# A four-layer graph network on one core: edge rows kept behind the node table, equal sources counted where sums to sources are made, shared segments stored in two transfers, and stores issued by ScalarE

## The reference, cut to what matters

```
L0  three times: h = h @ W_self.T + b + mean over dst of h[src] @ W_neigh.T   (relu after two of them)
L1  h = (mean over dst of (x[src]-e) @ W_O.T + mean over src of (x[dst]-e) @ W_I.T + x @ W_S.T + biases) / 3,
    then batch norm over all nodes
L2  message = h[src] @ W_msg.T + b + embedding[type], summed over dst; then a GRU cell on all nodes
L3  mean over src of (h @ W.T + b)[dst]
```

## Time and profile before

| | us |
|---|---|
| time of the kernel, median of 3 runs | 7199.35 |
| lowest and highest run | 7185.6, 7202.62 |
| the profiled execution's own time | 7203.87 |
| its span | 7202.2 |

### The profile page before, as it was taken

The page is one execution under the profiler, slowest core; times in us unless marked ns, Lnnn a source line. Parts: engine busy times, 40 slices in busy tenths (PEclk is TensorE's granted clock), DMA queues, the critical chain, the costliest instruction groups (busy, mean ns, idle before and its releaser), DMA issues. The chain is left out here.

```text
span 7202.2 us, 109209 instructions
## 1 busy us (share of the span) xinstructions
PE 4892.9 (68%) x23937; PEld 3564.2 (49%) x23937; DVE 4001.4 (56%) x14866; ACT 2898.1 (40%) x6394; POOL 4067.0 (56%) x4659
## 2 busy tenths in 40 slices
PE   4777745558788786723646536798999978844553
PEld 2455533445565565623543324576666644433553
DVE  5665555654564565733323216666999989943210
ACT  0565534443563463323001100246888855533000
POOL 0655556640550454666555650575888877755555
PEclk9888867679998998855778868557999989955776
DMA  2344446659667766934546537443444444433443
GB/s 85 126 143 135 138 142 189 192 165 333 214 223 290 240 223 206 299 127 135 155 131 145 103 50 229 132 130 131 171 171 170 171 138 147 123 104 123 81 71 47
DMA packets 730736, 1139.32 MB, mean 158 GB/s; under 512 B 109785, under 2 KB 426376, under 8 KB 730220
## 3 DMA queue, kind: packets, MB, share of 16 engines
q1 hardware_dynamic: 589770, 962.41, 40.0%
q0 software_dynamic: 140800, 175.08, 11.8%
HBM read 703.03 MB, written 456.06 MB: 161 GB/s over the span
## 5 line engine op out<-in xcount | busy, mean ns | idle before, releaser
L1061 POOL DMA_INDIRECT G_x<-node_table,G_idx x400 | 399.8, 999 | 165.6 <-issue 131.1
L1061 POOL DMA_INDIRECT G_V<-layer_rows,G_idx x400 | 381.3, 953 | 165.3 <-issue 98.0
L1915 PE MATMUL bank<-O_r,O_eq 125*125 125x128 f32 x1600 | 283.0, 359 | 242.5 <-ACT O_out L1941 210.3
L1091 PE MATMUL bank<-first_last_indicators,G_V 125*128 (+1 forms) x1600 | 282.8, 299 | 234.3 <-DVE G_V L1741 158.2
L1073 POOL DMA_INDIRECT out<-O_out,O_idx x200 | 314.4, 1572 | 211.5 <-DMA out<-O_out,O_idx 149.8
L1421 PE MATMUL bank<-B_S,B_V 127*128 127x125 f32 x2000 | 319.5, 302 | 148.2 <-DVE B_S L1409 104.6
L1073 POOL DMA_INDIRECT node_table<-H_out,H_idx x200 | 318.2, 1591 | 171.5 <-DMA node_table<-H_out,H_idx 116.0
L1915 PEld LDWEIGHTS bank<-O_r,O_eq 125*125 125x125 f32 x1600 | 275.6, 272 | 249.9 <-issue 166.7
L1091 PEld LDWEIGHTS bank<-first_last_indicators,G_V 125*128 125x128 f32 x1600 | 277.1, 261 | 244.4 <-issue 161.3
L1421 PEld LDWEIGHTS bank<-B_S,B_V 127*128 127x128 f32 x2000 | 276.2, 209 | 185.5 <-issue 154.7
L1058 POOL COPY G_idx<-i_tb 128x4 int32 (+1 forms) x100 | 18.5, 185 | 607.8 <-POOLq L255 483.6
(11 more groups left out here) (472 smaller groups left out, 15917.5 us busy)
## 6 DMA issues: line engine op xcount, KB each, us to landing
P_x<-node_table SPq DMA_DIRECT2D x196, 512.0 KB
B_V<-values SPq DMA_DIRECT2D x250, 256.0 KB
B_krow<-keys_dst SPq DMA_DIRECT2D x250, 250.0 KB
values<-G_V SPq DMA_DIRECT2D x200, 256.0 KB
BN_g<-node_table SPq DMA_DIRECT2D x195, 256.0 KB
out<-P_out SPq DMA_DIRECT2D x195, 256.0 KB
node_table<-G_xg SPq DMA_DIRECT2D x97, 512.0 KB
layer_rows<-A_a SPq DMA_DIRECT2D x100, 256.0 KB
```

What stands on the lines that cost most here:

```text
L1061: pool.indirect_dma_start(out=rows[u % len(rows)][:, c, :], out_offset=None, in_=table, in_offset=bass.IndirectOffsetOnAxis(ap=idx[u % len ...
L1091: last = nc.tensor.matmul(m.bank[7][:, bass.ds((i * TILE + c) * 2, 2)], V[0:EP, c, :], m.ind[0:EP, bass.ds(i * TILE + c, 1), :].rearrange( ...
L1915: last = nc.tensor.matmul(m.bank[2 + u % 2][0:EP, d * D:(d + 1) * D], eq[u][:, c, d * EP:(d + 1) * EP], r[u][:, c, :], start=(c == 0), sto ...
```

## The change

What it does, part by part:

1. **x1 rows behind the node table.** The table's memory grows to `XE`, 2N rows of 128 and behind them one group of 128 rows per tile, `X1`. B3's x1 is stored there in edge order by one dense transfer of 256 KB per body on SP; B3 has no POOL work any more. `i_src2` points at the source's X1 row where the source ends an edge, and at its row in the table otherwise; G3 gathers from XE. B4 loads x1 into the left half of `xg`, ACT writes g into the right half, and POOL scatters whole rows of 1 KB through `i_dstf`, so the destinations' x1 comes into the table here. Before, x1 went in B3 and g in B4, 512 B each.
2. **Equal sources.** The count behind `seen` moves from A to H. There DVE counts on the keys which H loads anyway, body by body, and writes the scatter's indices itself; POOL's index copy in H goes. `i_srcf`, which O2 uses, is made there too. A's `srow` loads go.
3. **Short stages.** Masks are taken with a stride (every fourth column, 50 at a time) so that the four tiles of a body come to lie side by side in one bank: 16 matmuls, 2 copies of 50 x 512, 2 transfers.
4. **Stores on ScalarE.** The queue that issues them changes for A's values, the layers' o (B1, B2), B3's h1 and h1T, and G4's V.
5. **Index copies.** `copy_index` is a call of its own. In A both copies stand ahead of the eight gathers. `next_index` copies the next body's index one body ahead, in G1, G2 and B5; for this it waits until the gathers of four bodies before have landed. Elsewhere the order is as before. B5's loop on POOL is unrolled 4 times instead of 8.

```diff
@@ edges_setup
-            nc.vector.tensor_scalar(m.i_src2[0:EP], csrc[:], 2.0, None, ALU.mult).then_inc(s_v, 1)
...
+            nc.vector.scalar_tensor_tensor(t1[:], csrc[:], -2.0, tb[:], ALU.mult, ALU.add).then_inc(s_f, 1)
+            dve.wait_ge(s_f, 5)
+            nc.vector.scalar_tensor_tensor(hi_f[:], t1[:], 2.0 * N, t2[:], ALU.add, ALU.mult).then_inc(s_f, 1)
+            dve.wait_ge(s_f, 6)
+            nc.vector.scalar_tensor_tensor(m.i_src2[0:EP], csrc[:], 2.0, hi_f[:], ALU.mult, ALU.add).then_inc(s_f, 1)
@@ index copies
+def copy_index(nc, index, idx, s_idx, g, w):
+    nc.gpsimd.tensor_copy(idx[w % 4][:], index[:, bass.ds(g * TILE, TILE)]).then_inc(s_idx, 1)
+def next_index(nc, f, index, idx, s_idx, g, w, landed):
+    if f.has(g):
+        f.landed(landed, g - 4, w % 4, 64)
+        copy_index(nc, index, idx, s_idx, g, w)
@@ share_segments
-                        nc.vector.tensor_copy(R[k][c][:], m.bank[4 * (1 - k) + c][0:TC, 0:D]).then_inc(s_r, 1)
+                    nc.vector.tensor_copy(R[k][:], m.bank[4 + k][0:T // TILE, :]).then_inc(s_r, 1)
...
-                    for c in range(2):
+                    for q in range(TILE):
                         for e in range(2):
-                            last = nc.tensor.matmul(m.bank[4 * (1 - k) + c][0:TC, 0:D], masks[e][:, c * TC:(c + 1) * TC],
+                            last = nc.tensor.matmul(m.bank[4 + k][0:T // TILE, q * D:(q + 1) * D],
+                                                    masks[e][:].rearrange("p (i c) -> p i c", c=TILE)[:, :, q],
...
-                            sp.dma_start(table[EP + k, c * TC // TILE:(c + 1) * TC // TILE, q, :], R[k][c][q:TC:TILE, :]).then_inc(s_out, 16)
+                    sp.dma_start(table[EP + k], R[k][:]).then_inc(s_out, 16)
@@ edges_start (A)
-                    gather(nc, pool, f, m.i_src, idx_s, s_is, i, u, a["x"], xs_whole, s_gs)
-                    gather(nc, pool, f, m.i_dst, idx_d, s_id, i, u, a["x"], xd_whole, s_gd)
+                    copy_index(nc, m.i_src, idx_s, s_is, i, u)
+                    copy_index(nc, m.i_dst, idx_d, s_id, i, u)
+                    gather(pool, f, idx_s, s_is, i, u, a["x"], xs_whole, s_gs)
+                    gather(pool, f, idx_d, s_id, i, u, a["x"], xd_whole, s_gd)
...
-                    sp.dma_start(srow[u][:], ks.to_broadcast([128, EG])).then_inc(s_sr[u], 16)
...
-                            nc.vector.scalar_tensor_tensor(hits[:, c, 0:e], srow[u][0:EP, 0:e], m.csrc[:, t], m.before[:, c, 0:e],
-                                                           ALU.is_equal, ALU.mult, accum_out=seen[:, t]).then_inc(s_c, 1)
@@ A, ScalarE (and alike in layer, third_layer, messages)
+                        Flow(act, has, m).after(s_h, i - 2)
+                        act.dma_start(value_tiles(m, i - 2), hs_whole[v][:]).then_inc(s_vo[v], 16)
@@ third_layer (B3)
+                    if has(i - 3):
+                        v = (u - 3) % 4
+                        Flow(sp, has, m).after(s_x1, i - 3)
+                        sp.dma_start(edge_rows(m.X1, i - 3), x1_whole[v][:]).then_inc(s_1o[v], 16)
...
-            @block.gpsimd
-            def _(pool):
...
-                        scatter(nc, pool, f, m.i_dst2f, idx, s_i, i - 3, (u - 3) % 4, m.XH, x1_whole, s_sc)
@@ outgoing_self (B4)
+                    Flow(sp, has, m).landed(s_sc, i - 4, u, 64)
+                    sp.dma_start(xg_whole[u][:, :, 0:D], edge_rows(m.X1, i)).then_inc(s_x[u], 16)
...
                     f.after(s_g, i)
+                    f.landed(s_x, i, u)
                     f.landed(s_sc, i - 4, u, 64)
-                    scatter(nc, pool, f, m.i_dst2f1, idx, s_i, i, u, m.XH, g_whole, s_sc)
+                    copy_index(nc, m.i_dstf, idx, s_i, i, u)
+                    scatter(pool, f, idx, s_i, i, u, m.XG, xg_whole, s_sc)
@@ add_to_src (H), VectorE
+                        f.after(s_seen, i - 1)
+                        for c in range(TILE):
+                            e = (c + 1) * EP
+                            last = nc.vector.scalar_tensor_tensor(hits[:, c, 0:e], krow[u][0:EP, 0:e], m.csrc[:, bass.ds(i * TILE + c, 1)],
+                                                                  m.before[:, c, 0:e], ALU.is_equal, ALU.mult, accum_out=seen[u][:, c:c + 1])
...
+                        f.landed(s_sc, i - 4, u, 64)
+                        nc.vector.tensor_scalar(later[u][:], seen[u][:], 0.5, float(1 << 22), ALU.is_gt, ALU.mult).then_inc(s_ix, 1)
...
+                        nc.vector.tensor_scalar(idx[u][0:EP], row[u][:], 1.0, None, ALU.add).then_inc(s_i, 1)
@@ gru (B5), GpSimd
+                    next_index(nc, g, m.i_dst, idx, s_i, i + 3, u + 3, s_x)
                     if has(i + 2):
-                        g = Flow(pool, has, m)
                         g.after(s["x2"], i - 2)
-                        gather(nc, pool, g, m.i_dst, idx, s_i, i + 2, (u + 2) % 4, m.XG, x_whole, s_x)
-
-                sweep(pool, -2, n, n + 4, body, unroll=8, back=7, ahead=2, special=0)
+                        gather(pool, g, idx, s_i, i + 2, (u + 2) % 4, m.XG, x_whole, s_x)
+
+                sweep(pool, -3, n, n + 4, body, back=7, ahead=3, special=0)
@@ network
+        m.XE = nc.dram_tensor("node_table", [2 * m.N + edge_rows_at_end, D], F32, kind="Internal").ap()
+        m.XH, m.X1 = m.XE[0:2 * m.N, :], m.XE[2 * m.N:, :]
```

More of the change, by code:

```diff
@@ L1486, in body @@
                         nc.scalar.activation(o[v][:], m.bank[2 + v % 2][:, 0:EG], ACT.Relu, bias=m.col[f"b{k}"]).then_inc(s_o, 1)
-                sweep(act, 0, n, n, body, back=5, ahead=0, special=0)
+                    if has(i - 2):
+                        v = (u - 2) % 4
+                        Flow(act, has, m).after(s_o, i - 2)
+                        act.dma_start(turned(H_out, i - 2), o[v][:]).then_inc(s_oo[v], 16)
+                sweep(act, 0, n, n + 1, body, back=5, ahead=0, special=0)
             @block.tensor
@@ L1525, in body @@
                 f = Flow(pool, has, m)
-                f.landed(s_vo, i - 4, u)
-                f.after(s_hl, i - 4)
-                gather(nc, pool, f, m.i_tb, idx, s_i, i, u, table, V_whole, s_g)
-            return 0, n, n - 1, 0, body
+                next_index(nc, f, m.i_tb, idx, s_i, i + 1, u + 1, s_g)
+                if has(i):
+                    f.landed(s_vo, i - 4, u)
+                    f.after(s_hl, i - 4)
+                    gather(pool, f, idx, s_i, i, u, table, V_whole, s_g)
+            return -1, n, n - 1, 0, body
         def sync(sp):
@@ L1655, in body @@
                         nc.scalar.activation(h1T[u][:], m.bank[4 + u % 2][:, 0:EG], ACT.Copy).then_inc(s_hT, 1)
-                sweep(act, 0, n, n + 3, body, back=8, ahead=0, special=0)
+                        Flow(act, has, m).after(s_h1, i - 4)
+                        act.dma_start(edge_rows(m.H1, i - 4), h1_whole[u][:]).then_inc(s_ho[u], 16)
+                    if has(i - 5):
+                        v = (u - 5) % 4
+                        Flow(act, has, m).after(s_hT, i - 5)
+                        act.dma_start(turned(m.HDb, i - 5), h1T[v][:]).then_inc(s_To[v], 16)
+                sweep(act, 0, n, n + 4, body, back=8, ahead=0, special=0)
             @block.tensor
@@ L1846, in _, with add_to_src @@
                 sweep(pe, 0, n, n, body, back=4, ahead=0, special=0)
-def add_to_src(nc, m, name, load, table, index, weight=None):
+def add_to_src(nc, m, name, load, table, weight=None):
     n = m.T // TILE
@@ L1861, in add_to_src @@
         idx = P.slots("idx", [128, TILE], I32)
+        if weight:
+            hits, seen = P.sb("hits", [EP, TILE, EG]), P.slots("seen", [EP, TILE])
+            later, row = P.slots("later", [EP, TILE]), P.slots("row", [EP, TILE])
+            s_seen, s_ix, s_pad = P.sem("seen"), P.sem("row"), P.sem("index_pads")
         s_l, s_e, s_k, s_sc = (P.sems(x) for x in ("r", "ea", "k", "out"))
@@ L1873, in body @@
                         sp.dma_start(ea_whole[u][:], attr_rows(m, i)).then_inc(s_e[u], 16)
-                    Flow(sp, has, m).after(s_eq, i - 4)
+                    Flow(sp, has, m).after(s_seen if weight else s_eq, i - 4)
                     keys = m.KS.rearrange("t p -> (t p)")[bass.ds(i * EG, EG)].rearrange("(a n) -> a n", a=1)
@@ L1951, in body @@
                     f.landed(s_sc, i - 4, u, 64)
-                    scatter(nc, pool, f, index, idx, s_i, i, u, table, out_whole, s_sc, add=True)
+                    if not weight:
+                        copy_index(nc, m.i_srcf, idx, s_i, i, u)
+                    scatter(pool, f, idx, s_i, i, u, table, out_whole, s_sc, add=True)
                 sweep(pool, 0, n, n - 1, body, back=4, ahead=0, special=0)
@@ L2073, in body @@
                         load(f, i + 3, (u + 3) % 4)
-                    if has(i - 4):
-                        f.after(s_v, i - 4)
-                        sp.dma_start(value_tiles(m, i - 4), V_whole[u][:]).then_inc(s_vo[u], 16)
-                sweep(sp, -3, n, n + 3, body, back=4, ahead=3, special=0)
```

(11 more changed lines are left out.)

145 lines of the change are left out of this document (62 added, 83 removed).

## The result

The changed kernel takes 7119.36 us (median of 4 runs, 7109.29 to 7132.73), the kernel before 7200.99 us beside it. The ratio is 0.9891, with a 95% interval of 0.9867 to 0.9914: 62 to 96 us faster. The forecast was 7064 us, a gain of 135 us; the measured time lies at the upper end of the range (the ratio, taken from the forecast's 7199.35 us, gives 7120.9 us), and the gain is six tenths of the one forecast. The profiled execution took 7115.8 us, its span 7114.1 us, 88.1 us less than before.

| stage | before | after | difference | forecast |
|---|---|---|---|---|
| B3 | 342.5 | 259.4 | -83.1 | -66 |
| A | 666.0 | 712.9 | +46.9 | -30 |
| five short stages | 86.9 | 58.3 | -28.6 | -24 |
| B5 | 478.3 | 444.0 | -34.3 | -21 |
| G1 + G2 | 734.5 | 703.2 | -31.3 | 0 |

A forecast was written before the change was run, and what follows sets the result against it. Each stage has its own limit: DMA bytes in B1 and B2, POOL's row of indirect transfers in A, B3 and B4, scatter landings in H. Terms -66 -30 -24 -21 +5 +2 -1 = -135 us give 7064 us, range 7020 to 7120.

The forecast's parts named there:

- One of the two long gaps becomes a short one: A: both index copies in front save POOL 0.51 us per body; taken as -16 us (0 to -26).
- PE may take part of it back: A: PE, at mean clock 0.67, needs 6.9 us a body, so the copy-order gain of 20 us was cut to 16.
- The 28.9 us of waits on ACT's h: A: POOL's waits for ACT's h, behind DVE; the count's leaving was to recover 6 us (0 to 20).
- The second term of A: A: removing the equal-source count gains 8 us in DVE's last bodies and 6 us of POOL's waits.
- the prediction's own sign: The forecast is wrong if B3 stays over 300 us, short stages don't fall, or an unchanged stage moves over 5 us.
- B3's own rate: B3: 350 transfers at 0.80 us give 279 us, 285 with ends; 276 us taken, -66 us (-88 to -42).
- The floor of 254 us: B3: at B1's 0.71 us per transfer the stage takes 254 us; with A at -50, a rival of 7022 us, 14%.
- three bodies, 17.7 us: B4: SP's slack while awaiting scatter i-4 covers the 16.1 us from first load to first scatter; +5 us (+2 to +35).
- Three bodies, 29 us, cover them: H: that slack hides DVE's new wait for scatter i-4; +2 us (-2 to +10).
- The wait for it goes: 0.53 us: B5: copying the index a body ahead saves 0.53 us in some 40 bodies, -21 us (-25 to 0).
- rival 3: B5 keeps its pace, +21 us, 7085 us, 12%; a DVE-GpSimd lock held for whole instructions would instead let DVE's wait shrink.
- rival 6: Stores block ACT where DMA is saturated in B1, B2 and B3: 7292 us, slower; 3%.

The follow-up runs named there:

- run 1: Changed kernel with A's index copies each before its own four gathers, B4 loading x1 a body later, G1's early copy undone: 7051.62 us, ratio 0.981.
- run 4: Changed kernel plus, in A, one unused small POOL copy and its wait between source and destination gathers: 7051.13 us, ratio 0.981, A 661.4 us.
- BN: The batch_norm stage, without POOL work in the changed kernel (237 us); with 160 unused gathers added: 434.4 us without gaps, 403.3 and 308.1 us with gaps.
- run 9: Changed kernel with the count back in A, old copy order; gap behind each added BN gather, extra gap in G1, G4's index copied ahead: 7108.34 us.
- run 5: Changed kernel with three gaps per body in A, B4's x1 load on ScalarE, H's index later, 160 gathers without gaps in BN: 7319.56 us.
- run 6: Changed kernel with A's old copy order and values stored by SP, 46 of B4's 50 x1 loads omitted, BN gathers with index copies: 7317.03 us.
- run 7: Changed kernel with A's old copy order and 40 dense loads in BN instead of gathers: A 690.0, B4 352.3 (unedited), BN 266.7 us.
- run 8: Changed kernel with gaps after every two gathers in A, B4's x1 load on ScalarE, H's index a body later: 7046.74 us, ratio 0.9812.
- run 2: Changed kernel with A's values stored by SP and H's index written behind the next body's eq and val: 7089.41 us, ratio 0.9854, H 539.9 us.

## Why the prediction was right and wrong

**A is the step that failed.** "One of the two long gaps becomes a short one: 0.51 us per body, in some 40 bodies of the loop 20 us" priced the copy right, even low (11.54 to 10.7 us). The error was to take POOL's issue for A's bound and its gaps for pure loss. Runs 1 and 4 show that the second long gap of a body is worth 49 to 52 us: with it POOL's waits for ACT's h, which needs TensorE's increments of four bodies before, are 31 to 45 us instead of 121. BN shows that gathers without gaps hold TensorE's readers up where nothing else binds the two. "PE may take part of it back" had the engine, but put it down to the clock; the granted clock is 0.67 in both kernels. The 28.9 us of waits on ACT's h were the hint; I booked them as a gain. So were two waits for TensorE's transposes in A of the kernel before ("remote" is a releaser that the profile can't name):

```profile
ACT A_h_srcT L1341 <- remote: 127.9, 29, 15.2
DVE A_h_dstT L1299 <- remote: 120.2, 29, 11.3
```

The second term of A, 14 us for the count, is worth nothing with two gaps (run 9: 660.7 with it, run 1: 663.8 without).

**G1 and G2, forecast 0, gave 31 us.** "POOL is busy 200 of 368 us there and its gathers wait for TensorE" is true and was, as I now read it, the reason to expect something: TensorE's increments in turn come late beside POOL's gathers. The body fell from 7.05 to 6.73 us. Run 1 shows that the copy ahead is the cause in G1; that the shorter POOL stretch frees the increments earlier is the reading that fits A and BN, not shown on its own. Run 9's G4 warns that the same edit does harm where POOL never stands. By the prediction's own sign, a stage called unchanged that moves by more than 5 us, G1 and G2 alone, with 16 us each, said that it was wrong.

**B3.** Right in kind, sized at B3's own rate. Its queues now:

```profile
q1 hardware_dynamic: 36000, 64.94, 69.2%
q10 hardware_dynamic: 14400, 25.91, 26.2%
```

350 transfers at 95.4% of 259.4 us are 0.71 us each, B1's price in the earlier trace rows; the 0.80 us were measured with scatters beside them. The floor of 254 us was the better choice, and the clock was no limit: the granted clock rose from 0.80 to 0.95.

**B4.** The wait on SP was named and priced at +5 with a bound of +35; it cost 15 to 17 us (runs 5, 6 against 7), in eight waits of POOL for g (one before, the start's). The "three bodies, 17.7 us" didn't cover the chain; that TensorE's late increments inside it are what was missing isn't shown on its own. The last 4 us over the kernel before (328.1 in run 8) are open; the start accounts for 2 (the first scatter is 21.1 instead of 18.9 us into the stage).

**H.** "Three bodies, 29 us, cover them" failed, +14 us. The trace after, POOL's last scatter of a body and the first of the next, with SP and DVE between:

```profile
3985.70 0.33 SPq L1871 DMA_DIRECT2D H_r<-h_of_dst  x1
...
3988.49 1.55 POOL L1082 DMA_INDIRECT node_table<-H_out,H_idx  x1 [0.30 <-issue]
...
3992.56 0.17 DVE L1906 TENSOR_SCALAR H_later<-H_seen 125x4 f32<-125x4 f32 x1 [5.19 <-DMA node_table<-H_out,H_idx]
...
3993.31 1.55 POOL L1082 DMA_INDIRECT node_table<-H_out,H_idx  x1 [3.27 <-DMA node_table<-H_out,H_idx]
```

DVE's wait for the landing of scatter i - 4 stands ahead of eq and val of the next body, so these and SP's loads come 3 us into the scatter instead of at its start, and the last scatter lands 2.5 us after the end of its issue. Taking the wait out of the way gave 13 us back (run 2), with a mean body of 10.15 us instead of 10.42 (10.08 before). That the loads' bytes delay the landing is my reading of these rows and not shown by itself.

**B5.** "The wait for it goes: 0.53 us" was 0.65, and 0.4 us came on top: POOL's small operation takes 1.04 us instead of 1.43. One gather is 0.15 us longer, so the body fell by 0.88 us, from 8.92 to 8.04. DVE's tensor_scalar shrank with it, from a mean of 1.51 to 0.84 us, as the lock in the prediction's rival 3 has it; whether POOL's operation or DVE's is the cause no run shows.

```profile
5986.90 0.19 POOL L1057 COPY B_idx<-i_dst 128x4 int32 x1
5987.27 1.04 POOL L1071 DMA_INDIRECT B_x<-node_table,B_idx  x1 [0.18 <-issue]
...
5992.70 1.04 POOL L2241 TENSOR_TENSOR B_rs<-B_ve,minus_half 125x4 f32<-125x4 f32 x1
```

**Short stages.** Right: 11.1 to 12.4 us each. 16 loads of 50 strided columns took 3.35 us, 0.21 us each, just what 8 loads of 100 adjacent ones took each in the earlier trace rows; neither the cost of the stride nor a gain from half the columns is there. The granted clock is 0.50 in the old row and 0.53 in the new; whether the load or the matmul sets the pace no run shows.

```profile
1668.16 3.35 PEld L1138 LDWEIGHTS bank<-A_shared_rows,later_tiles 100*50 100x50 f32 x16
```

**Stores on ScalarE, set-up**: 0, as forecast (B1 183.0 us; run 6). The prediction's rival 6 didn't happen.

## What to carry to other kernels

Before a gap on one engine is closed, look at what passes in it: a gap that costs its engine 0.8 us per body was worth 50 us of the stage. Where a matmul's recorded end and its consumer's start lie far apart with nothing between, read the increments' times, and try a gap in POOL's row of gathers, where POOL isn't the bound. How many is to be measured: in A one for four gathers gave 661 to 664 us and one for two 684 us on the first kind of chip, but 690 to 703 and 682 us on the second. A new wait on an in-order engine belongs behind the work of the next body, not ahead of it (H, B4).

## What the hardware did that I had not expected

While POOL issues plain indirect transfers back to back, TensorE's semaphore increments arrive late: by 5.8 us for the matmul shown in BN, by 0.01 us in the same stage with POOL idle or with the same bytes moved by dense loads. In A of the kernel before, the increment of a body's eight transposes follows that of the matmuls ahead of them by 0.91 us where POOL is idle and the clock full, and mostly by 2.2 to 5.0 us, in steps of some 0.7 us, while it gathers. In the changed kernel the increments that were held come together, two within 0.1 us, in 14 of its stalls, 2.4 to 2.8 us after the end of the last gather of the row. The Trainium skill, "TensorE: Matmul & The Clock Gate", section "The cost: per-tile semaphore tail", has increments of TensorE queue one behind the other at 26.3 ns each. The 0.01 us of the stages without gathers doesn't conflict with that; the lateness beside gathers is beyond it. In H and O2, where POOL's scatters add and are busy 58% of the time, increments are on time (0.01 us). Why those differ, and what part of the chip holds the increments, no run here shows.
